# Mamba scan in a decoder block: chunk-end carries in three stages, the turned input of an item two items ahead

## The reference, cut to what matters

```python
for i in range(2):                                  # two layers
    x = x + block(rmsnorm(x, norm_w[i]), ...)
# block, per batch row, 512 tokens, 512 channels (4 tiles of 128), 16 states:
xz = x @ in_w.T; xb, z = split(xz)
xb = silu(causal_conv4(xb) + cb)
delta, Bm, Cm = split(xb @ xp_w.T); delta = softplus(delta @ dtw.T + dtb)
dA = exp(delta[..., None] * -exp(a_log)); mi = delta[..., None] * Bm * xb[..., None]
v = 0.6 * v + mi                                    # over the tokens
h = dA * h + v
y = sum_n(h * C) + dp * xb
out = (y * silu(z)) @ ow.T
```

## Time and profile before

| | us |
|---|---|
| median of 3 runs | 1576.0 (1574.37 to 1579.76) |
| profiled execution, its own time | 1579.03 |
| its span | 1577.6 |
| TensorE matmuls busy | 1419.4 (90%) |
| VectorE busy | 1056.6 (67%) |
| GpSimd busy | 930.5 (59%) |
| ScalarE busy | 895.0 (57%) |
| first scan starts at | 84.96 |
| mean granted clock of TensorE | 0.955 |

### The profile page before, as it was taken

The page is one execution under the profiler, slowest core; times in us unless marked ns, Lnnn a source line. Parts: engine busy times, 40 slices in busy tenths (PEclk is TensorE's granted clock), DMA queues, the critical chain, the costliest instruction groups (busy, mean ns, idle before and its releaser), DMA issues.

```text
span 1577.6 us, 46812 instructions
## 1 busy us (share of the span) xinstructions
PE 1419.4 (90%) x20506; PEld 977.3 (62%) x20506; DVE 1056.6 (67%) x1339; ACT 895.0 (57%) x1277; POOL 930.5 (59%) x809
## 2 busy tenths in 40 slices
PE   4769999999999999999999987878989897999997
PEld 2347677577677677667667765633444343489996
DVE  3179898598698598688788776577666672332223
ACT  2567668577677677676666646216555556434440
POOL 1158898889899799889889886630303000035541
PEclk8679999999999999999999998869999999999999
DMA  4002212221222122221222245470424200712225
GB/s 149 31 28 83 82 59 80 82 82 57 90 102 78 61 83 83 82 83 57 82 84 82 96 140 130 81 147 1 73 49 74 34 1 1 274 41 68 71 68 177
DMA packets 41498, 127.29 MB, mean 81 GB/s; under 512 B 8784, under 2 KB 21584, under 8 KB 32848
## 3 DMA queue, kind: packets, MB, share of 16 engines
q1 hardware_dynamic: 34736, 108.29, 21.3%
q0 software_dynamic: 6048, 14.95, 3.6%
q10 hardware_dynamic: 512, 1.05, 0.4%
HBM read 97.91 MB, written 9.57 MB: 68 GB/s over the span
## 4 chain that ended last, share of the span: by engine, by line
PE 51%; DVE 27%; issue 8%; ACT 7%; POOL 3%; DMA 2%; SPq 2%; DVEq 0%; ACTq 0%
DVE hst L775 12%; PE psum L627 7%; PE psum L568 5%; PE psum L606 5%; PE psum L1704 4%; PE psum L1716 4%; PE psum L1292 4%; DVE overlay L675 3%; DVE w_early L775 3%; PE psum L513 2%; PE psum L1274 2%; POOL hst L981 2%; PE psum L1646 2%; PE psum L1258 2%; DVE nmax L1413 2%
## 5 line engine op out<-in xcount | busy, mean ns | idle before, releaser
L981 POOL TENSOR_TENSOR hst<-hst,cb 128x512 f32<-128x512 f32 x399 | 511.6, 1305 | 134.7 <-DVE hst L775 118.9
L775 DVE TENSOR_TENSOR_SCAN hst<-dA,psum 128x512 f32<-128x512 f32 x399 | 464.1, 1203 | 157.3 <-PE psum L627 157.1
L606 PE MATMUL psum<-ident,hst 128*128 128x128 f32 x1596 | 239.4, 285 | 16.0 <-POOL hst L981 13.2
L910 ACT ACTIVATE dA<-delta,alog 128x512 f32<-128x512 f32 x256 | 178.3, 720 | 88.3 <-DVE hst L775 68.3
L606 PEld LDWEIGHTS psum<-ident,hst 128*128 128x128 f32 x1596 | 176.8, 143 | 64.0 <-issue 25.1
L910 ACT ACTIVATE dA<-xres,alog 128x512 f32<-128x512 f32 x256 | 176.5, 719 | 64.0 <-DVE hst L775 50.4
L1413 DVE TENSOR_REDUCE nmax<-psum 128x2 f32<-128x1024 f32 x128 | 154.6, 1221 | 56.7 <-PE psum L1258 56.3
L1342 ACT ACTIVATE pT<-psum 128x1024 f32<-128x1024 f32 x128 | 127.9, 1024 | 102.4 <-PE psum L1278 78.0
L627 PE MATMUL psum<-filt,c_early 64*64 64x86 f32 (+1 forms) x6144 | 146.2, 240 | 20.7 <-DVE hst L775 10.9
L627 PE MATMUL psum<-filt,uT 64*64 64x86 f32 (+1 forms) x6144 | 145.6, 239 | 20.5 <-DVE hst L775 10.5
L627 PEld LDWEIGHTS psum<-filt,c_early 64*64 64x64 f32 x6144 | 125.5, 135 | 58.5 <-issue 42.6
(11 more groups left out here) (231 smaller groups left out, 2156.6 us busy)
## 6 DMA issues: line engine op xcount, KB each, us to landing
cb<-c_rows SPq DMA_DIRECT2D x64, 1024.0 KB, 4.8
qk_first<-w_early SPq DMA_DIRECT2D x64, 64.0 KB, 2.4
qk<-part SPq DMA_DIRECT2D x64, 64.0 KB, 2.6
w_up<-up_dram SPq DMA_DIRECT2D x8, 512.0 KB, 7.4
w_down<-down_dram SPq DMA_DIRECT2D x8, 512.0 KB, 13.9
w_up<-y_choice SPq DMA_DIRECT2D x8, 512.0 KB, 7.7
qk<-part POOLq DMA_DIRECT2D x48, 64.0 KB, 5.3
qk_first<-part SPq DMA_DIRECT2D x40, 64.0 KB, 2.4
```

The costliest lines, as they stand in the source:

```text
L606: m = pe.matmul(psum[:, Y0 + et % EP, t * P:(t + 1) * P], hst(i)[:, t * P:(t + 1) * P], ident[:], start=n == 0 and t == 0, stop=n == NSTAT ...
L775: dve.tensor_tensor_scan(hst(i), a, v, 0.0, ALU.mult, ALU.add).then_inc(scan_done, 1)
L910: act.activation(dA[:, a % NDA, :], delta[k % 2][:, et, :], ACT.Exp, scale=alog[:, k // B, et, n:n + 1]).then_inc(decay_done, 1)
L981: pool.tensor_tensor(h, h, cb[:, q % 2, state_of(i)[1] % GN, :], ALU.mult).then_inc(g_done, 1)
```

## The change

The stages `lo` and `hi` are replaced by three. Stage e1 makes the odd chunk ends (1, 3, 5) of the first half from all chunks before, each as two halves of 256 columns spread over the four column groups. Stage e2 makes the even ends (0, 2, 4) of the first half, each from one chunk and its carry row (one matmul of 512 columns in each of three groups), and beside it, on the rows of the second half, its odd ends 1 and 3 (256 columns, 3 as halves in two groups; 1 as 512 columns in the third). Stage e3 makes the even ends 0, 2, 4 of the second half. e1 and e3 use one bank, e2 two. `bend` shrinks to the three odd ends and one slot for "own chunk" per chunk: 384 elements a row where there were 576. ScalarE's copies become 6 (256 columns) after e1, 3 (512) and 3 (two of 256, one of 512) after e2, 3 (512) after e3. The stages stand at steps 50, 54, 58.

For items k = 3 to 7, xs moves to step 58 and xn to steps 60 and 61 of item k - 2, and p to 1, 5, 9, 13 of item k - 1. z moves to 37, 40, 43, 47 for all.

```diff
-LO_AT = ((5, 4, 3, 2), (None, None, 0, 1))
-HI_AT = ((4, 3, 2, 1), (None, None, 0, None))
-TILED = ("lo", "hi")
+OWN = 3
+E1 = ((0, 5, 0), (1, 5, 1), (2, 3, 0), (3, 3, 1), (2, 1, 1), (3, 1, 0))
+E2LO = E3 = ((0, 0, None), (1, 2, None), (2, 4, None))
+E2HI = ((0, 3, 0), (1, 3, 1), (2, 1, None))
+STAGES = {"e1": ((0, E1),), "e2": ((0, E2LO), (KT, E2HI)), "e3": ((KT, E3),)}
+TILED = tuple(STAGES)
...
-                    steps[engine].setdefault((at, s), []).append((k,) + name)
-                xn_at = 2 if k > 1 else start + 2
-                p_at = (6, 9, 12, 14) if k > 1 else range(start + 5, start + 5 + ET)
+                    steps[engine].setdefault((at, s) if s >= 0 else (at - 1, s + TILES), []).append((k,) + name)
+                xn_at = 60 - TILES if k > 2 else 2 if k > 1 else start + 2
+                p_at = (1, 5, 9, 13) if k > 2 else (6, 9, 12, 14) if k > 1 else range(start + 5, start + 5 + ET)
...
-                    put((38, 41, 45, 58)[m], "pe", "z", m)
-                    put((38, 41, 45, 58)[m] + 1, "act", "z", m)
+                    put((37, 40, 43, 47)[m], "pe", "z", m)
+                    put((37, 40, 43, 47)[m] + 1, "act", "z", m)
...
-                for part, s in (("lo", 50), ("hi", 56)):
-                    for n in range(2):
+                for part, s in (("e1", 50), ("e2", 54), ("e3", 58)):
+                    for n in range(len(STAGES[part])):
                         put(s, "pe", part, n)
                         put(s + n, "act", part, n)
...
-                    sides = [pe_open(k, what, n) for n in range(2)]
-                    if what == "lo":
+                    sides = [pe_open(k, what, n) for n in range(len(STAGES[what]))]
+                    if what == "e1":
                         pe.wait_ge(bend_done, k + 1)
                         pe.wait_ge(bank_act, emptied_by("act", k, "u", NCH - 1))
                     else:
-                        pe.wait_ge(bank_act, emptied_by("act", k, "lo", 1))
...
+                        pe.wait_ge(bank_act, emptied_by("act", k, *(("e1", 0) if what == "e2" else ("e2", 1))))
+                    sums = {}
+                    for bk, (r0, ends_of) in zip(sides, STAGES[what]):
+                        for g, end, half in ends_of:
+                            cols = slice(0, DI) if half is None else slice(half * HS, (half + 1) * HS)
+                            first = end if end % 2 == 0 else 0
+                            for c in range(first, end + 1):
+                                sums.setdefault((r0, g), []).append((bk, r0, g, cols, end, c, first))
+                    for turn in range(max(map(len, sums.values()))):
+                        for queue in sums.values():
+                            if turn < len(queue):
+                                bk, r0, g, cols, end, c, first = queue[turn]
+                                i = pe.matmul(bk[g * BC:g * BC + NSTATE, cols], bend[r0:r0 + KT, c, end // 2 if end % 2 else OWN, :], uT[par][r0:r0 + KT, c, cols],
+                                              start=c == first, stop=c == end, tile_position=(r0, g * BC))
+                    i.then_inc(bank_full, len(sides))
...
                     if i % TILES == 0:
-                        pe.wait_ge(bank_act, emptied_by("act", k, "hi", 1))
+                        pe.wait_ge(bank_act, emptied_by("act", k, "e3", 0))
...
+                    for g, end, half in ends_of:
+                        cols = slice(0, DI) if half is None else slice(half * HS, (half + 1) * HS)
+                        to, c = (r0, end + 1) if end < NCH - 1 else (KT, 0)
+                        i = act.copy(uT[par][to:to + NSTATE, c, cols], bank(k, what, j)[g * BC:g * BC + NSTATE, cols])
                     i.then_inc(bank_act, 1)
```

More of the change, by code:

```diff
@@ L212, in build @@
             toep = sb(mc, "toep", [P, QC])
-            ends = sb(mc, "ends", [P, NCH, NCH])
+            ends = sb(mc, "ends", [P, NCH, OWN + 1])
             keep = sb(mc, "keep", [P, 1])
@@ L228, in build @@
             bcol = sb(mc, "bcol", [P, 2, NCH, NSTATE])
-            bend = lay(NCH * P)[:, 0:NCH * NCH * NSTATE].rearrange("p (e c n) -> p e c n", e=NCH, c=NCH)
+            bend = lay(NCH * P)[:, 0:NCH * (OWN + 1) * NSTATE].rearrange("p (c e n) -> p c e n", c=NCH, e=OWN + 1)
             filt = sb(mc, "filt", [P, NFILT, NCH, 2, QC])
@@ L331, in plan_first @@
                 s += 1
-                for part in ("lo", "hi"):
-                    for n in range(2):
+                for part in STAGES:
+                    for n in range(len(STAGES[part])):
                         put("pe", part, n)
                     s += 1
-                    for n in range(2):
+                    for n in range(len(STAGES[part])):
                         put("act", part, n)
@@ L872, in act_side @@
                              bank(k, "u", j).rearrange("p (c e x) -> p c e x", c=2, e=ET)).then_inc(bank_act, 1)
[L873 to L878, removed]
+                elif what in STAGES:
+                    r0, ends_of = STAGES[what][j]
+                    act.wait_ge(bank_full, filled(k, what, len(STAGES[what]) - 1))
+                    for g, end, half in ends_of:
+                        cols = slice(0, DI) if half is None else slice(half * HS, (half + 1) * HS)
+                        to, c = (r0, end + 1) if end < NCH - 1 else (KT, 0)
+                        i = act.copy(uT[par][to:to + NSTATE, c, cols], bank(k, what, j)[g * BC:g * BC + NSTATE, cols])
                     i.then_inc(bank_act, 1)
@@ L930, in pool_side @@
                     if k:
-                        pool.wait_ge(bank_full, filled(k - 1, "hi", 1))
+                        pool.wait_ge(bank_full, filled(k - 1, "e3", 0))
                     else:
                         pool.wait_ge(ld_scan, 64)
-                    pool.tensor_tensor(bend, bcol[:, par].unsqueeze(1).to_broadcast([P, NCH, NCH, NSTATE]),
-                                       ends[:].unsqueeze(3).to_broadcast([P, NCH, NCH, NSTATE]), ALU.mult).then_inc(bend_done, 1)
+                    pool.tensor_tensor(bend, bcol[:, par].unsqueeze(2).to_broadcast([P, NCH, OWN + 1, NSTATE]),
+                                       ends[:].unsqueeze(3).to_broadcast([P, NCH, OWN + 1, NSTATE]), ALU.mult).then_inc(bend_done, 1)
                 elif what == "u":
@@ L2002, in shape_constants @@
         toep[:, NSTATE + s, s:] = BETA ** np.arange(QC - s)
-    ends = np.zeros((2, KT, len(CHUNKS), len(CHUNKS)), np.float64)
+    ends = np.zeros((2, KT, len(CHUNKS), OWN + 1), np.float64)
     for e, (last, wide) in enumerate(CHUNKS):
-        ends[:, :NSTATE, e, 0] = BETA ** (last + wide)
         for c, (t0, width) in enumerate(CHUNKS[:e + 1]):
-            ends[:, NSTATE:NSTATE + width, e, c] = BETA ** (last + wide - 1 - t0 - np.arange(width))
-    toep, ends = toep.reshape(P, QC), ends.reshape(P, len(CHUNKS), len(CHUNKS))
+            if e % 2 or c == e:
+                at = e // 2 if e % 2 else OWN
+                if c == 0 or at == OWN:
+                    ends[:, :NSTATE, c, at] = BETA ** (last + wide - t0)
+                ends[:, NSTATE:NSTATE + width, c, at] = BETA ** (last + wide - 1 - t0 - np.arange(width))
+    toep, ends = toep.reshape(P, QC), ends.reshape(P, len(CHUNKS), OWN + 1)
     keep = (np.arange(P) % KT >= NSTATE).astype(f)[:, None]
```

4 lines of the change are left out of this document (2 added, 2 removed).

## The result

Slower, by half a per cent: 1583.9 us (median of 12 runs) against 1575.4 (12 runs of the kernel before), ratio 1.0052, interval 1.0027 to 1.0077. The forecast was 1551, range 1534 to 1568. Rival C had named 1584 to 1588, but from longer stages, which did not come; that its number was met is chance.

A forecast was written before the change was run, and what follows sets the result against it. TensorE's full queue was taken to make VectorE's scans late. Terms: 38.2 - 6.8 - 10.8 - 2.2 + 8.1 = 26.5 us off, giving 1552.5 from the profiled time or 1549.5 from the median; forecast 1551, range 1534 to 1568.

The forecast's parts named there:

- Rival C: Stages e1 and e2: a 256-column record takes nearly a 512-column one's time; 8 us slower, 1584 to 1588; chance 0.08.
- part 3: Items 3 to 7, xs, xn and p earlier: costs 10.8 us plus 2.2 for the fill of 10/11; spread convolutions nothing.
- Part 2: z at 37, 40, 43, 47: longer waits in steps 42 to 50, cost 6.8 us.
- Part 1: Three stages for two at steps 50, 54, 58, with z gone from 58: gain 38.2 us over seven items.
- part 4: The front, before the first scan: shorter stages bring the first fill at 74.7 instead of 82.8, gain 8.1 us.
- D: After e2 and e3: ScalarE's copies become the limit and take the gain back; no change, about 1576 us; chance 0.04.
- B: GpSimd becomes the bound and state adds begin to wait for products; 1564 us; chance 0.14.
- A: The moves of part 3 are free and the more regular banks help; gain 39.5 us, about 1538; chance 0.22.

## Why the prediction was wrong

| term | forecast | measured |
|---|---|---|
| front | 8.1 sooner | 8.0 |
| three stages, z left at 58 (38.2 less z's 12) | 26 gained | 38 less the front's 8 = 30 |
| z early (12 won at 58, 6.8 lost) | 5 gained | 10.6 lost, 5.5 of them the two stops in e1 |
| xs and xn two items ahead | 5 x 1.4 = 7 lost | 10.5 lost by the medians, 7.5 by the items' lengths |
| p early: p 0 at 1, the fill of 10/11 | 5 x 0.75 + 2.2 = 6 lost | 27 lost |
| of these, silu block and last convolution | 0 | 20 |

- **The step that failed** is in part 3: "The convolutions spread out cost nothing (VectorE has the same sum, and TensorE has two fills, adds and p, 5.9, in four steps against VectorE's four scans and a convolution, 6.7)". Both sums are right, and the engine that they leave out is ScalarE. Its silu block makes no decays for 6.4 us, and VectorE's five decays last 5.6; the difference was covered by the convolution that VectorE did between them. Moved ahead of scan 15, which the block waits for, the convolution covers nothing: 2.0 us on VectorE, 1.8 on TensorE, and in four of five items a halved clock that took 1.5 to 3.2 us more. A term put at nothing measured 20 us: the place of the silu alone undoes them, and that of p 3 undoes 24 in all. The rest of the 27 is what the prediction did count, 0.65 for p 0 in five items and 0.74 for the fill of 10/11 in four, where it had 0.75 and 0.55.
- For the transposes and for p 0 the prediction asked what hides the moved piece. For the convolutions it did not ask what the moved piece itself hid.
- **Part 2** had the waits of an early z right and their balance wrong. For odd items I set them against the 7.1 us that the odd items of the kernel before lose; with the three stages alone every item loses only 5.4 there, so what spoils the odd items, by the plan the order of banks, goes away with the stages and is no credit to the early z. The two stops in e1 (5.5 us in the profiled execution) have nothing like them in the `lo` of the kernel before.
- **Part 1 and part 4** held to some tenths in the waits behind the stages and in the front; 256 columns take about half of 512 (48 records in 2.78, 12 a group: 0.23 each), so rival C falls. Behind the first scan TensorE waited for ScalarE's copies once, 1.58 us ahead of e3 beside item 0, where the roots of a normalisation and two table loads of 1.28 us stand ahead of e2's copies; part 1 had no wait there, with 0.3 to spare, and the prediction named such a wait as a sign of being wrong. The item still came out 4.0 us shorter (forecast 4.2), and in no other item was ScalarE late for e2 or e3, so D falls. B falls as well: GpSimd's waits did not vanish. A falls: the transposes cost what was forecast, if e3 is ahead of them, and nothing beside the old `hi`. That the gain with z left at 58 is 30 and not 26 is in part the odd items' waits of steps 42 to 50, 5.4 us where there were 6.9, which no term has; the rest stays open.
- The range failed because the bounds of each term were taken on terms that had one, and a term of "nothing" got none.

## What to carry to other kernels

Before a piece is moved, ask what it hides: name the longest block on each of the other engines that runs beside it, what stock (here five decays) carries its neighbour over that block, and which event starts it. If the piece is moved ahead of that event, its whole time comes out of the cover. And an engine with side work to spare in sum can still be the one that is late, because its side work comes in one block.

## What the runs showed of the hardware

- After an idle time of 1.8 us on TensorE, in a stretch where it is otherwise busy over nine tenths, the granted clock was at half (1.2 GHz) for 3 to 7 us. So it was in four of five items of the changed kernel (in the fifth, TensorE idled 1.31 us and the clock stayed), in all five with six decay buffers (one of them after 1.39 us) and in three of five with only the moves, where the other two idled 1.8 us too and kept full clock. After 0.2 or 0.6 us at this place it never fell. What decides between the two was not tried.
- TensorE stopped in the e1 of item 3, behind its third record and with no wait in the profile, in the profiled execution of all seven builds with z at 37, 40, 43, 47, for 0.30, 0.57, 0.57, 1.25, 1.31, 1.76 and 1.93 us. Where it stopped for 1.25 or more, VectorE then waited 6.7 to 8.2 us and the clock halved behind the stop; where for 0.57 or less, 3.4 to 3.6, at full clock. In the e1 of item 5 the same seven builds stopped for 0.18 to 0.78 us. VectorE waited 3.3 to 3.8 us behind it at full clock, but 5.4 in the run with dbc at 19, where the clock halved behind a stop of 0.72 us; in two other builds it stayed full after 0.78. With the stages alone and with z at 36 both e1 ran through, though the former stopped for 0.72 us in the e1 beside item 0. That the stop is tied to the place of the instruction in the program is a guess; no run moved it alone.
